# Edge attention on one core: partial sums of all tiles kept in SBUF, padded rows, q staged by TensorE, and the small copies moved from ScalarE to VectorE

## What is computed

```python
x = x + _L0_gnn_ref(_layernorm(x), edge_attr_8, Wq, Wk, Wv, Wo, src, dst)
# q = (nfeat @ Wq.T) / SCALING, k = nfeat @ Wk.T, v = nfeat @ Wv.T, each (n, 8, 32)
# attn = einsum('ehd,ehd->eh', k[src], q[dst]) + attn_bias
# a    = exp(attn - segment_max(attn, dst)[dst]);  a = a / segment_sum(a, dst)[dst]
# out  = segment_sum(v[src] * a[:, :, None], dst) @ Wo.T
```

## Time and profile before

| | |
|---|---|
| median of 3 runs | 4279.67 us (4276.35 to 4288.94) |
| span of the profiled execution | 4287.7 us |
| its own time | not listed apart; of the three runs 4288.94 is the nearest, 1.2 us over the span |
| attention loop, first gather to the next phase's first gather | 220.45 to 1602.23 us |
| busy in the whole span | PE 70%, DVE 58%, POOL 48%, ACT 25% |
| gathers of kv rows | 928, 8 for a body |

### The profile page before, as it was taken

How to read it: one execution, slowest core, us unless ns; L and a number is a source line. 1 busy time by engine, 2 the same in 40 slices (tenths; PEclk the granted TensorE clock), 3 DMA queues, 4 the chain that set the end, 5 groups by cost and what they waited for, 6 DMA issues and landing times. The chain is left out here.

```text
span 4287.7 us, 49015 instructions
## 1 busy us (share of the span) xinstructions
PE 2980.3 (70%) x13743; PEld 2189.0 (51%) x13743; DVE 2479.7 (58%) x4593; ACT 1089.2 (25%) x2192; POOL 2064.3 (48%) x1781
## 2 busy tenths in 40 slices
PE   4335545544455545485688867999979897899798
PEld 2211211111111114364588856777758886688686
DVE  8457777777777764443699964111125666534443
ACT  1111111111111112121155542333334554100221
POOL 4666666666666642544387318888820000001233
PEclk7666776776766766698799987999989998999899
DMA  2466666666666647444266647456532443355433
GB/s 96 149 184 192 196 197 189 195 191 190 193 193 193 192 135 253 135 68 91 60 230 170 159 186 110 13 13 13 6 44 88 139 132 121 132 181 175 124 65 53
DMA packets 317791, 583.65 MB, mean 136 GB/s; under 512 B 100508, under 2 KB 221600, under 8 KB 308736
## 3 DMA queue, kind: packets, MB, share of 16 engines
q0 software_dynamic: 160880, 294.23, 31.7%
q1 hardware_dynamic: 137552, 235.63, 16.9%
q10 hardware_dynamic: 19264, 52.66, 3.9%
HBM read 421.02 MB, written 163.96 MB: 136 GB/s over the span
## 5 line engine op out<-in xcount | busy, mean ns | idle before, releaser
L2157 PE MATMUL gnn_p_msg<-gnn_msg,gnn_ident 128*128 128x512 f32 x928 | 678.0, 898 | 766.6 <-issue 458.0
L2110 POOL DMA_INDIRECT gnn_got<-kv,gnn_index x928 | 882.5, 951 | 455.5 <-issue 290.4
L2157 PEld LDWEIGHTS gnn_p_msg<-gnn_msg,gnn_ident 128*128 128x128 f32 x928 | 260.1, 294 | 1183.8 <-issue 1156.2
L2231 DVE TENSOR_TENSOR gnn_prod<-gnn_got,gnn_p_both 128x2048 f32<-128x2048 f32 x116 | 265.4, 2288 | 232.5 <-issue 190.2
L2537 POOL DMA_INDIRECT weight_table<-cell_of,cell_at x192 | 316.9, 1651 | 94.2 <-issue 50.0
L2537 POOL DMA_INDIRECT count_table<-cell_of,cell_at x192 | 315.0, 1641 | 68.0 <-issue 55.5
L2703 PE MATMUL tables_p_pair<-tables_spread,tables_hot 128*128 128x100 f32 x2816 | 335.4, 278 | 17.0 <-DVE tables_spread L2677 12.1
L2703 PEld LDWEIGHTS tables_p_pair<-tables_spread,tables_hot 128*128 128x128 f32 x2816 | 323.4, 193 | 28.7 <-DVE tables_spread L2677 20.3
L799 DVE SCALAR_TENSOR_TENSOR ffn_acc<-ffn_pC,ffn_gates,ffn_acc 128x256 f32<-128x256 f32 x200 | 88.9, 480 | 394.4 <-PE ffn_pC L643 384.5
L2245 DVE TENSOR_TENSOR gnn_msg<-gnn_got,gnn_p_both 128x2048 f32<-128x2048 f32 x116 | 264.7, 2282 | 72.8 <-ACT gnn_p_both L2138 40.2
L2964 PE MATMUL gnn_p_sum<-gnn_hs,gnn_edge 128*128 x2500 | 286.6, 277 | 15.4 <-DVE gnn_edge L2993 15.0
(11 more groups left out here) (445 smaller groups left out, 4703.0 us busy)
## 6 DMA issues: line engine op xcount, KB each, us to landing
slabs<-weight_table SPq DMA_DIRECT2D x25, 1600.0 KB
weight_table<-tables_weight_slab SPq DMA_DIRECT2D x11, 3200.0 KB
count_table<-tables_count_row SPq DMA_DIRECT2D x11, 3200.0 KB
gnn_cell<-count_table ACTq DMA_DIRECT2D x50, 576.0 KB
state<-gnn_out SPq DMA_DIRECT2D x116, 136.0 KB
ffn_xs<-by_expert SPq DMA_DIRECT2D x60, 260.0 KB, 3.3
gnn_got<-kv,gnn_index POOLq DMA_INDIRECT x928
gnn_cell<-count_table ACTq DMA_DIRECT2D x25, 448.0 KB
```

Source lines behind the costliest of these rows:

```text
L2110: pool.indirect_dma_start(out=got[k][:, r, :], out_offset=None, in_=kv_dram, in_offset=rows_at(index[k][:, r:r + 1])).then_inc(gathered[k] ...
L2157: last = nc.tensor.matmul(p_msg[k][:], ident[:], msg[k][:, r:r + 2].rearrange("p r h d -> p (r h d)"), start=(r == 0), stop=(r == R - 2))
L2231: dve.tensor_tensor(prod[v][:, :, :, 0:HD], keys, over(p_q[v], wide, "p (a h d) -> p a h d", a=1, h=HEADS), ALU.mult)
```

## The change

- kv rows grow from 512 to 528 floats and q rows from 256 to 264: each head gets a 33rd number, set to 1.0 once in `og`. ACT copies into the 32 others with a stride. The message of the 33rd number is then the weight itself, and its sum over the edges the sum of the weights.
- The sums of all tiles stay in SBUF (`acc`, 26 x 272 floats a partition). The peak of a tile is read and written in `acc`; `first`, `out`, `weight`, `weight_sum` and `msg` go. Messages are written over the values in `got[k]`.
- PE stages q: a matmul of q's 256 columns with SCALE times the identity, two bodies ahead, behind the wait for `msg_ready`. It sums the messages with eight matmuls of 264 columns in place of four of 512, and their end (`summed[k]`) is now what releases the set to POOL.
- ACT has two exponentials in a body, and no register load.
- DVE takes over the row numbers (`find_index`), the copy of the peak, and the bias as an addition to the scores; it loads four numbers into registers in each body (two tile numbers, two pieces). It drops the weights' sum and its addition, and adds PE's result in one instruction of 264 elements.
- SP stores each tile once, when `done_at` says that it is finished.

```diff
-        og = [s.sb(f"og{v}", [P, GROUP, 3 * F]) for v in range(2)]
+        og = [s.sb(f"og{v}", [P, GROUP, 3 * MSG]) for v in range(2)]
...
+                for v in range(2):
+                    pool.memset(og[v][:].rearrange("p t (h d) -> p (t h) d", d=HD + 1)[:, :, HD], 1.0)
...
-                    act.activation(og[g % 2][:, t, :], po[at % 2][:, 0:3 * F], ACT.Copy).then_inc(tile_out, 1)
+                    to = og[g % 2][:, t, :].rearrange("p (h d) -> p h d", d=HD + 1)
+                    act.activation(to[:, :, 0:HD], po[at % 2][:, 0:3 * F].rearrange("p (h d) -> p h d", d=HD),
+                                   ACT.Copy).then_inc(tile_out, 1)
...
+        acc = s.sb("acc", [P, TILES + 1, STATE])
...
-                    for k in range(SETS):
-                        b = g * SETS + k
-                        t = sp.value_load(tile_of[0:1, bass.ds(b, 1)], min_val=0, max_val=TILES)
-                        sp.wait_ge(out_ready, b + (LAG + 1))
-
-                        sp.wait_ge(stored, 16 * b + 16 * SETS)
-                        sp.dma_start(state_dram[bass.ds(t * P, P), :], out[k][:]).then_inc(stored, 16)
-                sp.wait_ge(stored, group_count(sp) * (16 * SETS) + 16 * SETS)
...
+                for t in range(TILES):
+                    finished = sp.value_load(done_at[0:1, t:t + 1], min_val=1, max_val=TILES * MAIN + LAG)
+                    sp.wait_ge(out_ready, finished)
+                    sp.dma_start(state_dram[t * P:(t + 1) * P, :], acc[:, t, :]).then_inc(stored, 16)
+                sp.wait_ge(stored, 16 * TILES)
...
-                        wait_apart(released[k], g + 1)
+                        wait_apart(summed[k], g + 1)
...
-                def find_index(b, k):
-                    at = piece(b)
-                    act.activation(index[k][:], source[:, bass.ds(at * R, R), 0], ACT.Copy).then_inc(index_ready, 1)
-
-                def stage(b, v):
-
-                    at = piece(b)
-                    act.activation(p_q[v].rearrange("p (a n) -> p a n", a=1), q[:, bass.ds(at // MAIN, 1), :],
-                                   ACT.Copy, scale=SCALE)
-                    act.activation(prod[v][:, :, :, HD], bias[:, bass.ds(at * R, R), 1:EDGE], ACT.Copy).then_inc(staged, 1)
-
...
-                        act.activation(p_weight[v], score[v][:, 0:R, :].rearrange("p r h -> p (r h)"),
+                        act.activation(p_weight[v][:, 0:R * HEADS], score[v][:, 0:R, :].rearrange("p r h -> p (r h)"),
                                        ACT.Exp).then_inc(weights_ready, 1)
-
-                        act.activation(score[1 - v][:, R, :], peak[k], ACT.Identity, bias=first[:, bass.ds(b + 1, 1)])
-                        act.activation(keep[k][:], score[v][:, R, :], ACT.Exp)
-                        act.activation(weight[k][:], score[v][:, 0:R, :], ACT.Exp).then_inc(keep_ready, 1)
-                        stage(b + 1, 1 - v)
-                        find_index(b + SETS, k)
+                        act.activation(keep[k][:], score[v][:, R, :], ACT.Exp).then_inc(keep_ready, 1)
...
+                def stage(b, v):
+
+                    rows_of = q[:, bass.ds(piece(pe, b) // MAIN, 1), :].rearrange("p a (h d) -> p (a h) d", h=HEADS)
+                    nc.tensor.matmul(p_q[v][:, 0:F], scaled[:], rows_of[:, :, 0:HD], start=True, stop=True).then_inc(staged, 1)
...
-                        for r in range(0, R, 2):
-                            last = nc.tensor.matmul(p_msg[k][:], ident[:],
-                                                    msg[k][:, r:r + 2].rearrange("p r h d -> p (r h d)"),
-                                                    start=(r == 0), stop=(r == R - 2))
-                        last.then_inc(summed, 1)
+                        b, v = g * SETS + k, k % 2
+                        pe.wait_ge(msg_ready, b + 1)
+                        stage(b + 2, v)
+                        for r in range(R):
+                            last = nc.tensor.matmul(p_msg[k][:, 0:MSG], ident[:], got[k][:, r, MSG:2 * MSG],
+                                                    start=(r == 0), stop=(r == R - 1))
+                        last.then_inc(summed[k], 1)
...
+                def find_index(b, k):
+                    dve.tensor_copy(index[k][:], source[:, bass.ds(piece(dve, b) * R, R), 0]).then_inc(index_ready, 1)
...
-                    dve.memset(score[0][:, R, :], -BIG)
-                    for k in range(SETS):
-                        dve.memset(out[k][:], 0.0)
-                        dve.memset(keep[k][:], 0.0)
+                    dve.memset(tile_of[:, 0:LAG], TILES)
...
-                def by_head(ap):
-                    return ap[:, 0:MSG].rearrange("p (h d) -> p h d", h=HEADS)
-
-                def keep_part(k):
-
-                    dve.tensor_reduce(weight_sum[:], weight[k % SETS][:].rearrange("p r h -> p h r"), AX.X, ALU.add)
-                    dve.tensor_tensor(by_head(out[k % SETS]), by_head(out[(k - 1) % SETS]),
+                def sums_of(t):
+                    return acc[:, bass.ds(t, 1), 0:MSG].rearrange("p a (h d) -> p (a h) d", h=HEADS)
+
+                def peak_of(t):
+                    return acc[:, bass.ds(t, 1), MSG:STATE].rearrange("p a h -> p (a h)")
+
+                def tile_at(b):
+
+                    return dve.value_load(tile_of[0:1, bass.ds(b, 1)], min_val=0, max_val=TILES)
+
+                def fade(t, k):
+                    dve.tensor_tensor(sums_of(t), sums_of(t),
                                       over(keep[k % SETS][:], [P, HEADS, HD + 1], "p (h a) -> p h a", a=1), ALU.mult)
 
-                def add_sums(k, count):
-
-                    of = by_head(out[k % SETS])
-                    halves = p_msg[k % SETS][:].rearrange("p (r h d) -> p r h d", r=2, h=HEADS)
-                    dve.drain()
-                    dve.tensor_tensor(of[:, :, HD], of[:, :, HD], weight_sum[:], ALU.add)
-                    dve.wait_ge(summed, count)
-                    for i in range(2):
-                        dve.tensor_tensor(of[:, :, 0:HD], of[:, :, 0:HD], halves[:, i], ALU.add)
-                        last = dve.drain()
-                    last.then_inc(out_ready, 1)
+                def add_sums(t, k, times):
+
+                    dve.wait_ge(summed[k % SETS], times)
+                    dve.tensor_tensor(sums_of(t), sums_of(t),
+                                      p_msg[k % SETS][:, 0:MSG].rearrange("p (h d) -> p h d", h=HEADS), ALU.add)\
+                        .then_inc(out_ready, 1)
 
                 plan()
+                for k in range(SETS):
+                    find_index(k, k)
+                dve.wait_ge(const_loaded, 16)
+                dve.tensor_scalar(scaled[:], ident[:], SCALE, None, ALU.mult).then_inc(scaled_ready, 1)
+                dve.memset(acc[:, :, 0:MSG], 0.0)
+                dve.memset(acc[:, :, MSG:STATE], -BIG)
+                dve.drain()
...
+                        keys = got[k][:, :, 0:MSG].rearrange("p r (h d) -> p r h d", h=HEADS)[:, :, :, 0:HD]
+                        values = got[k][:, :, MSG:2 * MSG].rearrange("p r (h d) -> p r h d", h=HEADS)
                         dve.wait_ge(gathered[k], g * (16 * R) + 16 * R)
                         dve.wait_ge(staged, b + 1)
...
+                        dve.tensor_tensor(prod[:], keys, over(p_q[v][:, 0:F], [P, R, HEADS, HD], "p (a h d) -> p a h d", a=1, h=HEADS),
+                                          ALU.mult)
+                        t, late = tile_at(b + LAG), tile_at(b)
+                        at = piece(dve, b)
+                        dve.tensor_copy(score[v][:, R, :], peak_of(t))
+                        find_index(b + SETS, k)
                         dve.drain()
                         dve.tensor_reduce(score[v][:, 0:R, :].rearrange("p r h -> p (r h)"),
-                                          prod[v][:].rearrange("p r h d -> p (r h) d"), AX.X, ALU.add)
-                        dve.drain()
-                        dve.wait_ge(keep_ready, b + 1)
-                        dve.wait_ge(stored, 16 * b + 16)
-                        dve.tensor_reduce(peak[k], score[v][:].rearrange("p r h -> p h r"), AX.X, ALU.max)
-                        dve.drain()
-                        dve.tensor_tensor(score[v][:], score[v][:], over(peak[k], [P, R + 1, HEADS], "p (a h) -> p a h", a=1),
+                                          prod[:].rearrange("p r h d -> p (r h) d"), AX.X, ALU.add)
+                        dve.drain()
+                        dve.tensor_tensor(score[v][:, 0:R, :], score[v][:, 0:R, :], bias[:, bass.ds(at * R, R), 1:EDGE], ALU.add)
+                        dve.drain()
+                        dve.tensor_reduce(peak_of(t), score[v][:].rearrange("p r h -> p h r"), AX.X, ALU.max)
+                        dve.drain()
+                        dve.tensor_tensor(score[v][:], score[v][:], over(peak_of(t), [P, R + 1, HEADS], "p (a h) -> p a h", a=1),
                                           ALU.subtract).then_inc(shifted, 1)
```

(27 more changed lines are left out.)

80 lines of the change are left out of this document (26 added, 54 removed).

## The result

The changed kernel takes 4295.54 us (median of 20 runs) and the kernel before 4280.43 (20 runs): the ratio is 1.003, with a 95% interval of 1.0017 to 1.0042. The forecast was 4107. The ratio is that of the fast runs: one of the 20 runs of the changed kernel took 4569.65 us at a lower granted clock (0.727 for 0.85) and is left out of it. So a change that takes work from ACT and SP and shortens DVE's body gives nothing, and costs a third of a per cent.

The account below looks back on a forecast made before the run. It took POOL's gathers (10.0 us a body) plus 1.7 us from ACT's instruction stream to bound the attention loop. With T = 10.2, 115 T + 36.5 gave 1209.5 us, 172.3 less: 4107 us, range 4080 to 4225.

Parts of the forecast that it names:

- the other 1.7 us a body: Attention loop: body time beyond POOL's 10.0 us, put down to ACT's instruction stream, whose two late jobs the change removes.
- T of 10.2: Time of one attention-loop body after the change: DVE and POOL equal at 10.0 us, with the port 10.2.
- Rival 6: Slow stretches come from POOL's or DMA's load and still delay ACT and SP: T near 11.7, no change; chance 0.03.
- it is late nowhere: PE in the loop: under 10.0 us a body, its sums needed only two bodies later, its set four bodies later.
- cover of 7.7 us: Spare time in a set's 30 us between gathers, after landing, DVE and PE fill 22.3 us.
- Rival 5: Slow stretches move with the register loads to DVE, costing 1200 us: 5500 us in all; chance 0.03.
- Rival 1: POOL alone paces the loop: T 10.02, loop 1188.8 us, 4087 us in all; chance 0.53 together with the forecast.
- The port: DVE instructions with two SBUF operands hold up POOL's gathers: 0.15 us a body, bounds none to 0.4.
- 0.22 to 0.45: Sign that the forecast is right: the time in us of each of PE's instructions in the loop.
- 9.88: DVE's body after the change, in us: 9.48 before, plus and minus its changed parts; 10.0 with the branch.
- The loads, +0.85: DVE's four register loads behind the product delay the reduction by 0.85 us; bounds +0.2 and +2.9.

Follow-up runs that it names:

- e1_no_loads: The changed kernel with no register load left in DVE's loop, tile and piece worked out from the loop's counter: 4318.02 us.
- e2_index_act: The changed kernel with the row numbers' copy and its register load moved back to ACT, behind its exponentials: 4295.39 us.
- r2_after: The changed kernel, unaltered, run again on chip D as the reference of that group: 4283.78 us.
- e16_act_loads_again: The changed kernel with six more register loads a body on ACT, results unused, run again on chip D: 4297.01 us.
- e8_act_loads: The changed kernel with six more register loads a body on ACT, behind its exponentials, results unused, on chip B: 4075.24 us.

## Why the prediction was wrong

**The step that failed** is in the third paragraph: "the other 1.7 us a body come from somewhere else: from ACT's instruction stream". The rows behind it were read rightly, but what they show is a link and not the source. ACT was late, and POOL did wait for it (each stop ended 0.9 us behind ACT's copy). But eight gathers a body come at no more than about 0.69 a us on such a chip, and ACT's and SP's register instructions are only where this showed first. With ACT's two jobs gone the slow instructions came on DVE and POOL waited for PE's late signals, and with DVE's loads gone (`e1_no_loads`) the signals alone are left. Each time the stops came to nearly the same total: 164 to 193 us in some 1340. The 1.7 us a body were not ACT's to give back, so the sum's T of 10.2 was 1.55 us too small: it was 11.75. Rival 6 was what happened, T 11.75 for "near 11.7", though on DVE and PE rather than on ACT and SP; I gave it 0.03, because I took the unfailing order (slow load, late number, POOL waits) for the cause. Two things should have warned me. The text itself says it: "What starts these stretches the rows don't say". And in the stop of the earlier trace rows the trace of before has SP's register instructions as slow as ACT's, 0.70 us each, though neither waits for the other.

**A second step**, "it is late nowhere", failed with it. PE's work was sized rightly, and its cover of 7.7 us would have hidden it; but on a chip with stops PE's signals came up to 15 us late, and the change had made one of them what releases a set to POOL. Whether stops would be fewer in a kernel where DVE's signal releases the set, as before, was not tried; the kernel before loses 176 us by ACT instead.

**Rival 5** saw that the slow stretches would move to DVE and priced them at 1200 us, as if each load brought its own delay. Their sum hardly changed (176.4 to 192.7 us), and DVE was not what POOL waited for.

**The sums, taken for themselves, were good.** POOL: 1.25 us apart, 953 ns each for rows of 2112 bytes. Rival 1 gave 1188.8 us for the loop with POOL as the pace; on chip B it took 1189.4 with the changed kernel and six idle loads more. (The whole took 4075.24 and not 4087, as the work behind the loop was shorter there too: 2657.2 us for 2688.9 in the profile of after.) The port, priced at 0.15 us a body, shows as 953 for 951 ns, 0.02 us a body. PE's sums: 584.7 / 1856 = 0.315 us an instruction, 5.0 us a body, inside "0.22 to 0.45".

**DVE** was sized too dear: 9.88 for 8.96. The loads, +0.85, cost +0.20, the lower bound: product to reduction is 2.56 us against 2.36.
**What the change is worth where POOL leaves room** can be read from the runs with four gathers: the median body takes 8.93 us against 9.49 in the kernel before. Its loop took 1071.7 us and that of the kernel before 1132.6: 61 us (on chips A and B, neither with stops in that run). The work behind the loop is not in these. With eight gathers the gain is idle time on a chip like B (10.03 us a body in POOL) and is lost in the stops on the four others. That the two kernels are equal on B was not seen directly: 4075.24 for the changed one with the extra loads, 4069.45 for the one before.

**Why it is slower by 0.3%.** Two pairs ran on one chip each (C, E), and the third is that of the two profiles shown at first. From the first gather to the last the changed kernel needs 22.5, 19.9 and 13.7 us more. The tail to the next phase is 11.1, 5.5 and 12.3 us shorter, and the work behind the loop some 4 us longer each time (3.4 to 4.1). The stops themselves are longer: 190.3 us against 164.5 on chip E. About half of the longer gather time may go with the 2000 more instructions, PE's 16 sums a body and DVE's register work: on one chip each, 1789 more cost 10.3 us (`e1_no_loads` to `e2_index_act`) and 2160 more 10.9 (`r2_after` to `e16_act_loads_again`), so 5 to 6 ns each, 10 to 12 us here. That this is a cause is argued from two differences and not shown; the rest of the 20 us I can't assign.

**What stays open** is what the core counts. It isn't bytes, rows or packets: the kernel before moves 89,900 packets in that time and the one after 77,400, and the former is faster. By a straight line through the table a gather instruction weighs about 1.35 us and another some 10 ns (5 to 14 ns by pairs of runs on one chip), with residuals up to 20 us. I had no second chip like B to say what differs. The Trainium skill (NOTIFIC — the notification-queue block, section "7.1 Overflow: three behaviours, one of which stalls the engine") says that the block which writes the trace records always holds its producers back rather than lose a record inside. Pauses with no transfer in flight would look like that. Every run here has its trace, so none shows how the kernel goes without one, and that wasn't tried. But the traces point that way: the four of chip B hold each of the 16 signals that a gather's or store's landing gives, and no engine's signal is late in them. In the loops of all the others with seven or eight gathers only 16 to 30% of these landing signals are recorded, with four gathers on chip A 69%, and behind the loop 80 to 83%. So where the trace loses most records the core stops, and where it loses none it doesn't. That is a coincidence in twenty traces and not a proof: both could come from one thing that differs between the chips. If it is the recording, a part of what was measured here, and of the gap between the chips, belongs to the profile and not to the kernel.

## What to carry to other kernels

When an engine waits for a late partner, ask also what would stop it if the partner were early: sum its idle time, and look whether what it waited for was late only in stretches in which some other rate, here 0.69 gathers a us, is at its ceiling. Before a large change, cut the suspected load in half instead (four gathers of eight: one line) and see whether the stretches go. And run the kernel before beside every experiment: four runs on a faster chip would otherwise have seemed to prove a false theory. Where an engine waits and the profile names nobody, look also at whether the trace is complete.

## What the runs showed of the hardware

- The kernel before takes 4069 us on one chip (one run) and 4268 to 4317 on four others. The changed kernel with six loads more issues 0.80 gathers a us on the first and 0.69 on another (`e8_act_loads`, `e16_act_loads_again`).
- On such chips engines lose time in pieces of 0.7 us on instructions of their sequencers (register work, branches, drains): ACT and SP in the kernel before (some 500 each in one loop), DVE in the one after (some 370), nobody on chip B (at most 3).
- In the same loops PE's signals come up to 15 us late in the profile of the changed kernel (99 of 172 recorded ones over 1 us) and up to 21 us in `e1_no_loads`; on chip B, and with four gathers a body on chip A, at most 0.02 us.
- In the profile of the changed kernel a run of gathers that has such pieces lasts 9 to 22 us, mostly 15 to 17, before the first one comes (one run of 48, which followed a stop of 1.1 us, apart).
- A gather of 64 rows takes POOL 903 to 909 ns in the mean and one of 128 rows 947 to 959: most of its price is that of the instruction.
- Four register loads with their address work and two small copies behind one DVE instruction of 2.28 us put off the next big one by only 0.20 us.
